# One load split in two: ids and place by a 32-byte DMA, values by a 3584-byte DMA, in the statistics stage of a graph network

## The reference, cut to what matters

```python
z = jnp.concatenate([node_feats[src], node_feats[dst], edge_feats], axis=1)
gate = jax.nn.sigmoid(_bn(z @ W_int + b_int, g_int, be_int))
upd = jax.nn.softplus(_bn(z @ W_upd + b_upd, g_upd, be_upd))
agg = jax.ops.segment_sum(gate * upd, dst, num_segments=N_NODES)
```

## Time and profile before

| | |
|---|---|
| median of 3 timed runs | 12520.16 us (12508.35 to 12523.67) |
| span of the profiled execution | 11406.2 us |
| the rest of the median, outside the span | 1113.96 us |
| the stage for statistics, in the span | about 3294 to 4210 us |
| DMA engines' share in its steady part (3310 to 4180 us) | 0.95, at 259 GB/s |
| PE, DVE and ACT busy in these 870 us | 870.0, 858.5 and 632.2 us |

### The profile page before, as it was taken

One profiled execution on the slowest core, in us unless ns is written; L12 is line 12 of the kernel. 1 busy time (PEld: TensorE's weight loads), 2 busy tenths in 40 slices (PEclk: granted clock), 3 DMA queues, 4 the chain that ended last, 5 costly groups with the idle time before them and its releaser, 6 DMA issues. The chain is left out here.

```text
span 11406.2 us, 450173 instructions
## 1 busy us (share of the span) xinstructions
PE 8435.7 (74%) x151967; PEld 7165.3 (63%) x151980; DVE 8731.5 (77%) x21856; ACT 6239.0 (55%) x14764; POOL 4892.2 (43%) x5061
## 2 busy tenths in 40 slices
PE   6444444389989988997776787778887788776876
PEld 6444444388867768887656667457674576754854
DVE  6777777678889989995675785976868768688367
ACT  0222222189977769996205536975369763597410
POOL 1777777634420001110560470733717437265055
PEclk9999999989999989997998989999899998998998
DMA  5555553279989979995976998969989689896996
GB/s 208 178 178 179 179 173 89 67 262 332 331 267 258 258 214 307 322 322 191 332 248 227 294 277 294 317 231 291 275 296 314 222 298 273 288 318 225 382 325 227
DMA packets 1297371, 2928.48 MB, mean 257 GB/s; under 512 B 381130, under 2 KB 925444, under 8 KB 1272162
## 3 DMA queue, kind: packets, MB, share of 16 engines
q1 hardware_dynamic: 956302, 1976.15, 50.3%
q0 software_dynamic: 296704, 823.09, 24.2%
q10 hardware_dynamic: 44116, 125.96, 4.0%
HBM read 1753.51 MB, written 1104.99 MB: 251 GB/s over the span
## 5 line engine op out<-in xcount | busy, mean ns | idle before, releaser
L563 POOL DMA_INDIRECT rows_s<-place_rec,place_index x1568 | 1506.2, 961 | 537.7 <-issue 524.3
L645 PE MATMUL place_slot_ps<-place_runs,place_oh_turned 50*128 50x100 f32 x3136 | 728.6, 424 | 1108.3 <-ACT place_oh_turned L597 1096.4
L2476 POOL DMA_INDIRECT hop_x<-cols_all,hop_index x864 | 987.9, 1143 | 1017.9 <-ACT hop_index L2483 749.3
L645 PEld LDWEIGHTS place_slot_ps<-place_runs,place_oh_turned 50*128 50x128 f32 x3136 | 683.0, 327 | 1138.8 <-issue 1125.9
L2492 ACT ACTIVATE hop_parts<-hop_x,mask 128x64 f32<-128x64 f32 x5184 | 1258.5, 337 | 3.4 <-DMA hop_x<-cols_all,hop_index 3.3
L2539 PEld LDWEIGHTS hop_sums_ps<-hop_parts,hop_onehot 128*128 128x128 bf16 x18144 | 586.1, 97 | 646.4 <-issue 646.2
L2539 PE MATMUL hop_sums_ps<-hop_parts,hop_onehot 128*128 128x64 bf16 x18144 | 687.0, 192 | 327.0 <-DVE hop_parts L2521 313.6
L1630 POOL DMA_DIRECT2D cm_onehot<-hot_d x288 | 152.7, 531 | 1778.0 <-POOLq L107 978.3
L2281 POOL DMA_INDIRECT mask_cols<-cols_all,mask_index x432 | 425.3, 984 | 1000.8 <-ACT mask_index L2305 899.0
L2278 POOL DMA_INDIRECT mask_cols<-cols_all,mask_index x432 | 667.3, 1545 | 250.0 <-ACT mask_index L2305 155.1
L606 ACT COPY place_rec<-keys 128x32 f32 x98 | 21.5, 220 | 1362.4 <-DMA place_rec<-in_e 1354.8
(11 more groups left out here) (443 smaller groups left out, 28513.6 us busy)
## 6 DMA issues: line engine op xcount, KB each, us to landing
cols_all<-att_in_rows SPq DMA_DIRECT2D x216, 896.0 KB
mask_onehot<-hot_s SPq DMA_DIRECT2D x108, 1792.0 KB
cols_all<-hop_in_rows SPq DMA_DIRECT2D x216, 896.0 KB
hop_onehot<-hot_s SPq DMA_DIRECT2D x864, 224.0 KB
rows_all<-blank SPq DMA_DIRECT2D x72, 1808.0 KB
ct_u<-rows_all SPq DMA_DIRECT2D x288, 452.0 KB
cm_v<-rows_all SPq DMA_DIRECT2D x288, 448.0 KB
cm_onehot<-hot_d POOLq DMA_DIRECT2D x288, 448.0 KB
```

What stands on the lines that cost most here:

```text
L563: nc.gpsimd.indirect_dma_start(m.rows_s.rearrange("p n w -> (p n) w"), bass.IndirectOffsetOnAxis(index[:, j, t:t + 1], 0), rec[:, j, t, :] ...
L645: last = nc.tensor.matmul(slot_ps[b][:, t, 0:2 * NBK], oh_turned[:, b, t, :], runs[:, b, t, :], start=True, stop=True)
L2476: nc.gpsimd.indirect_dma_start(x[:, n, :, :].rearrange("p c f -> p (c f)"), None, table, bass.IndirectOffsetOnAxis(index[:, n:n + 1], 0)). ...
```

## The change

The tile `u` keeps the 896 values alone. A second tile, `ids`, takes the 7 ids and the place number. A load is two DMAs on the same queue, the 32 bytes of each partition first and the 3584 bytes after it, and both count to the same semaphore, so that the wait before `hots` asks for 32 where it asked for 16. What reads ids or place reads them from `ids`.

```diff
-        u = sb("u", [P, 6, UW])
+        u = sb("u", [P, 6, C * W])
+        ids = sb("ids", [P, 6, C + 1])
...
                 def load(it, n):
-                    sp.dma_start(u[:, n, :], m.rows_d[:, bass.ds(it, 1), :].rearrange("p b w -> p (b w)")).then_inc(came[n], 16)
+                    rows = m.rows_d[:, bass.ds(it, 1), :].rearrange("p b w -> p (b w)")
+                    sp.dma_start(ids[:, n, :], rows[:, C * W:UW]).then_inc(came[n], 16)
+                    sp.dma_start(u[:, n, :], rows[:, 0:C * W]).then_inc(came[n], 16)
...
-                    dve.wait_ge(came[n % 6], (k * 2 + n // 6) * 16 + 16)
+                    dve.wait_ge(came[n % 6], (k * 2 + n // 6) * 32 + 32)
...
-                    nc.vector.tensor_tensor(onehot[:, i, :, :], b2(m.iota_p[:], BATCH), b3(u[:, n % 6, C * W:C * W + C], P),
+                    nc.vector.tensor_tensor(onehot[:, i, :, :], b2(m.iota_p[:], BATCH), b3(ids[:, n % 6, 0:C], P),
                                             ALU.is_equal).then_inc(hot, 1)
...
-                    nc.vector.tensor_tensor(v[:, i % 2, :, :], v_ps[i % 2][:], u[:, n % 6, 0:C * W].rearrange("p (c w) -> p c w", w=W),
+                    nc.vector.tensor_tensor(v[:, i % 2, :, :], v_ps[i % 2][:], u[:, n % 6, :].rearrange("p (c w) -> p c w", w=W),
                                             ALU.add).then_inc(valued, 1)
...
-                    nc.scalar.copy(place[:, bass.ds(it, 1)], u[:, (s * 4 + i) % 6, C * W + C:UW])
+                    nc.scalar.copy(place[:, bass.ds(it, 1)], ids[:, (s * 4 + i) % 6, C:C + 1])
```

## The result

The changed kernel takes 12539.65 us (median of 20 runs, 12512.27 to 12556.81), the kernel before 12514.42 us (20 runs, 12499.28 to 12533.48). The ratio is 1.0016, with a 95% interval of 1.0010 to 1.0023: slower by 20 us, between 12 and 29 us (the two medians lie 25 us apart). The 20 us lie just under the 25 us that the prediction called the limit of what can be told from no change, and with 20 runs on either side they can be told.

The account below looks back on a forecast made before the run. PE was taken to set the pace at 3.117 us a batch, with the chain over `hot_d` about as long. A later landing, 32 us, plus 1 us at the start took 12520 to 12553 us; range 12508 to 12610.

Parts of the forecast that it names:

- PE's beat and the full chain: Statistics stage: PE sets 3.117 us a batch; the three-batch loop through SP's queue and `hot_d` is within 0.2 us of it.
- The added issue on SP delays what follows: SP's queue after the squares: values load, `hot_d` and `turned_d` all go out 0.46 us later.
- The shift of the landing: `hot_d` store lands 0.10 to 0.56 us later, taken as 0.33; a third, 0.11 us a batch, 32 us over 287.
- The slack of the chain: `hot_d` loop against PE's beat: 0 to 0.2 us in three batches could take off 0 to 19 us; nothing taken.
- The start of the stage: Six more issues before the first `hots`: it comes some 0.5 us later, 1 us at most with the first store.
- the sum of 33 us: Whole kernel: 32 us from the later `hot_d` landing plus 1 us at the stage's start.
- The short packets: DMA engines: 128 packets of 32 bytes a batch, eight per engine at 12.9 ns, add 0.10 us of engine time.
- One turn a batch: DMA queue: alternating loads and stores costs 0.9 us a batch once, since two loads in a row share it.
- two turns: Rival, DMA queue: the split load costs another 0.9 us, engines need 4.00 us a batch, 12773 us; chance 0.09.
- the turn is a fixed 0.9 us: DMA engines: of 2.96 us a batch, 2.0 are bytes and 0.9 the alternation of loads and stores.
- What lies outside the span: Whole kernel: 1114 us of the median lie around the profiled span of 11406.2 us and stay untouched.
- The signs in the profile: Profile after: `hots` every 3.23 us, `hot_d` waits in most batches, PE gaps 0.1 us, DMA engines 3.06 us a batch.

Follow-up runs that it names:

- Cutting the chain in the kernel before: Kernel before with the `hot_d` store of batch it+1 issued ahead of SP's wait for the squares and the load; 12603.89 us, ratio 0.9998.
- cutting it in the changed kernel: Changed kernel with the `hot_d` store of batch it+1 issued before SP's wait for the squares of batch it; 12516.34 us, ratio 0.9998.
- the other order: Changed kernel with a batch's two loads swapped, the 3584 bytes first and the 32 bytes behind them; 12511.93 us, ratio 0.9999.

## Why the prediction was right, point by point

**PE's beat and the full chain.** Right. Cutting the chain in the kernel before left 3.117 us, and cutting it in the changed kernel gave them back. The 8 waits of 1.4 us in total were the only sign of it in the list of waits, and they were enough to look for.

**The added issue on SP delays what follows.** Right. The prediction had 0.46 us from the six issues in a row. In the loop it is 0.54: the values go out 0.72 us after the squares where it was 0.18. In the loop SP runs an ALU_OP of 37 ns and a MOVE of 29 ns for that line besides the issue of 355 ns. What has to go out later is the load of the values; with the store of `hot_d` alone late, as in the other order, nothing was lost.

**The shift of the landing, 0.33 us as the middle of 0.10 and 0.56.** The mechanism was right, and the size too. Over the steady part the store of `hot_d` goes out 0.56 us later after the squares (on average 1.32 us where it was 0.76), and its round trip is 0.25 us shorter (4.78 where it was 5.03), so it lands 0.31 us later. That the middle of two bounds came so near is luck: the prediction had no reason for the middle, and the trace doesn't say which engine lands last.

**The slack of the chain, taken as nothing.** This term of the sum was the one that was off. Three batches got 3 x 0.073 = 0.22 us longer, not 0.31. The mean distance between the landing and its use fell by 0.05 us (0.19 to 0.14), and that from the one-hot instruction to `v` by 0.04 us (1.044 to 1.008): 0.31 - 0.05 - 0.04 = 0.22. The prediction had seen that the slack could be worth 0 to 19 us; it was worth some 9. The start of the stage was taken as 1 us; the first one-hot instruction came 5.1 us after the first load's issue where it had been 3.6. So the sum of 33 us should have been 30 - 9 = 21 us, and 22 with the start.

**The short packets, 0.10 us of engine time a batch.** The term was too large and mattered less than the prediction thought. The records of the 32-byte packets give 9 ns each, 0.07 us for eight, and the engines' time went from 2.96 to 2.99 us a batch, since the values' packets took less. Put where SP is idle, the packets cost nothing at a share of 95.2%. So the read-modify-write of which the Trainium skill warns (DMA: Bandwidth & Descriptors, Specifications) may be done here, but no cost of it can be seen.

**One turn a batch, shared by the two loads.** Right: with two turns the engines would have needed 4.0 us. The fixed cost of about 2 us a DMA that the Trainium skill gives (DMA: Bandwidth & Descriptors, Anatomy of one DMA) is stated there for DMAs that GpSimd issues, which the prediction left out; these are issued by SP. It is no time of the queue in these runs: with the ids' DMA the engines' time a batch is 0.03 us longer.

**That the turn is a fixed 0.9 us.** Wrong, without harm to the number. It shrinks when one more issue stands between the load and the stores, to some 0.6 us (last section).

**What lies outside the span.** Wrong: 1.5 to 3.3 us, not 1114. The difference of the two times was read as a part of every execution, when it was a difference between executions. The sum was of differences inside the stage, so it didn't suffer.

**The signs in the profile.** The 128 packets, the later `hot_d` and DVE's waits for it came as described, with 3.190 us where 3.23 was given. PE's gaps came too, but make 5.4 us in 272 batches, 0.02 us each where 0.1 was given. "In most batches" was too much for the list of waits, which has 32 + 62 of 272; but in the trace's events the one-hot instruction follows the landing by 0.12 us in the middle batch, the least distance that occurs, and by under 0.2 us in 254 of 272 batches. In the kernel before it was so in 191 of 279, where the list has 8 waits: it leaves out gaps of up to 0.15 us, so few waits in it don't mean that few batches wait. The engines' time is 2.99 us a batch where 3.06 was given.

## What to carry to other kernels

A DMA issue that is added behind a wait delays everything that its queue issues after it. Its price is what of that delay reaches the end of the tightest chain through the queue, less the chain's slack, divided by the number of batches that the chain spans: here 0.54 us of issue became 0.31 us of landing, 0.22 us of chain and 0.07 us a batch. The same issue cost nothing behind the load of the values, though the stores still went out late, and nothing behind the stores. A few short waits for a DMA in a stage with a full PE are worth following around their loop before anything is put on the queue. And compare the span of a profiled execution with its own device time, not with the median of others.

## What had not been expected of the hardware

The time that the DMA engines lose with loads and stores in turn depends on when the stores are issued. With the stores 0.54 us behind the load, the share was 0.95 at 258 to 259 GB/s; with one more issue between, even of a single packet, 0.86 to 0.88 at 259 to 260 GB/s, and the stores landed 3.3 to 3.9 us after their issue where it had been 5.07. The packet records say where the time sits: in the packets of the values, while those of the stores stay at 41 and 74 ns. A packet of 3616 bytes takes 141 ns in the middle and 252 ns on average in the kernel before, which for the eight of an engine makes 0.89 us a batch over the middle value; with one more issue between, the average is 207 to 218 ns and the excess 0.53 to 0.61 us. Here it gains nothing, because PE's beat holds. What in the engines makes the difference stays open.
